# Earlier loads and clears, an overlapped first count tile, and edge groups of three in a graph layer kernel

## What is computed

```python
xn = layernorm(x)
# two graph convolutions; A counts the edges src->dst, plus one self loop for each node
def gcn_conv(x, W, b):                       # deg: edges and loop that end in a node
    norm = dinv[src] * dinv[dst]             # dinv = 1 / sqrt(deg)
    return segment_sum((x @ W.T)[src] * norm, dst) + b
gnn = gcn_conv(relu(gcn_conv(xn, W1, b1)), W2, b2)
# linear attention with exponential features, 12 heads of 64, 256 features
mix = layernorm(xn + attention(xn) @ W_proj + b_proj) * gamma + beta
x = x + gnn + mix
x = x + expert_ffn(layernorm(x))             # 8 experts, one chosen per row
```

## Time and profile before

| what | us |
|---|---|
| median of three runs | 2721.11 (2715.38 to 2743.76) |
| the profiled execution's own time | 2723.26 |
| its span | 2721.5 |
| PE busy | 2408.9 |
| DVE busy | 1390.2 |
| ACT busy | 798.5 |
| POOL busy | 796.1 |

### The profile page before, as it was taken

How to read it: one execution, slowest core, us unless ns; L and a number is a source line. 1 busy time by engine, 2 the same in 40 slices (tenths; PEclk the granted TensorE clock), 3 DMA queues, 4 the chain that set the end, 5 groups by cost and what they waited for, 6 DMA issues and landing times. The chain is left out here.

```text
span 2721.5 us, 44665 instructions
## 1 busy us (share of the span) xinstructions
PE 2408.9 (89%) x16483; PEld 1629.3 (60%) x16483; DVE 1390.2 (51%) x2868; ACT 798.5 (29%) x1090; POOL 796.1 (29%) x562
## 2 busy tenths in 40 slices
PE   2888989999999999998892899999998889999476
PEld 1666858676866666665561466666664556666354
DVE  5565848584666766765210444444441334444343
ACT  2223424332364654743110222222220001111132
POOL 1115444444455555554554000000000000000265
PEclk9989999999999999999996899999998999999688
DMA  5995545454412123123212666666656655444185
GB/s 216 384 380 143 136 127 136 133 152 111 119 1 59 1 58 58 0 59 67 61 0 54 221 215 215 218 220 217 218 196 224 216 171 168 169 167 162 42 162 107
DMA packets 161756, 392.18 MB, mean 144 GB/s; under 512 B 74832, under 2 KB 81850, under 8 KB 152028
## 3 DMA queue, kind: packets, MB, share of 16 engines
q1 hardware_dynamic: 77196, 299.90, 32.2%
q0 software_dynamic: 73632, 61.04, 12.9%
q10 hardware_dynamic: 10800, 29.50, 2.8%
HBM read 226.03 MB, written 169.83 MB: 145 GB/s over the span
## 5 line engine op out<-in xcount | busy, mean ns | idle before, releaser
L364 PE MATMUL pair<-arena 128*128 128x384 f16 (+2 forms) x5760 | 905.6, 319 | 25.0 <-SPq L353 7.9
L1744 PE MATMUL pair<-arena 128*128 128x384 f16 x4900 | 822.8, 328 | 84.1 <-DVE arena L1332 57.6
L675 POOL DMA_INDIRECT cells<-arena x392 | 637.3, 1626 | 631.5 <-DMA cells<-arena 456.3
L364 PEld LDWEIGHTS pair<-arena 128*128 128x128 f16 (+1 forms) x5760 | 566.9, 99 | 349.1 <-issue 25.1
L1744 PEld LDWEIGHTS pair<-arena 128*128 128x128 f16 x4900 | 476.6, 98 | 396.1 <-DVE arena L1332 58.0
L707 POOL DMA_INDIRECT slots<-arena x25 | 29.0, 1159 | 1022.2 <-DVEq L1447 1006.1
L1567 PE MATMUL pair<-arena 128*128 128x256 f32 x600 | 168.9, 416 | 17.5 <-ACT arena L779 17.5
L1578 PEld LDWEIGHTS pair<-arena 128*128 128x128 f32 x1200 | 159.6, 201 | 27.3 <-ACT arena L803 22.0
L1578 PE MATMUL pair<-arena 128*128 128x66 f32 x1200 | 159.3, 282 | 17.7 <-ACT arena L803 17.6
L1123 DVE SCALAR_TENSOR_TENSOR arena<-arena 128x256 f16<-128x256 f32 x392 | 161.8, 480 | 4.7 <-DVE arena L1051 4.4
L803 ACT ACTIVATE arena<-pair 128x512 f32<-128x512 f32 x150 | 87.2, 590 | 170.4 <-PE pair L1567 167.1
(11 more groups left out here) (191 smaller groups left out, 2274.0 us busy)
## 6 DMA issues: line engine op xcount, KB each, us to landing
cells<-arena POOLq DMA_DIRECT2D x25, 1600.0 KB, 11.6
arena<-cells SPq DMA_DIRECT2D x25, 1600.0 KB, 9.1
ahl_dram<-arena SPq DMA_DIRECT2D x25, 1600.0 KB, 12.4
arena<-ahl_dram SPq DMA_DIRECT2D x25, 1600.0 KB, 7.8
arena<-in_x SPq DMA_DIRECT2D x70, 384.0 KB
arena<-key_dram SPq DMA_DIRECT2D x28, 896.0 KB
split_w<-arena SPq DMA_DIRECT2D x32, 384.0 KB
arena<-split_w SPq DMA_DIRECT2D x32, 384.0 KB, 5.6
```

What stands on the lines that cost most here:

```text
L364: ins = nc.tensor.matmul(dst[half], left(k, a), right(k, b, half), start=start and n == 0, stop=stop and n == 2)
L675: nc.gpsimd.indirect_dma_start(cells, bass.IndirectOffsetOnAxis(ap=idx_all[:, m:m + 1], axis=0), val_all[:, m:m + 1], None, bounds_check=C ...
L1744: ins = nc.tensor.matmul(pair[u][:, half, 0:HD], a[:, 0, s * P:(s + 1) * P], X[part][:, s, half * HD:(half + 1) * HD], start=(s == 0 and p ...
```

## The change

It has five parts.

1. **Start.** All six weight blocks have their own staging place and are loaded at once. `consts` is raised to 1 as soon as the identity matrix is there, and only PE waits for that; DVE and ACT wait for the rest (`consts` 2) later. ACT loads its table early. Lo parts are transposed into bank 6, and ACT evicts the first three of them (`LO_ACT`).
2. **Clear.** The zero fill starts when the last weight block has landed, instead of when it has been split. The zeros' place moves from `xT`'s fourth chunk to its fifth.
3. **Loops.** The 24 DMAs of self loops go. POOL adds the identity to the diagonal block of each table tile in SBUF, for tiles 14 to 24; ACT's `counts` waits for `loops`. The reduction for the flag moves ahead of the last two scattered units.
4. **First count tile.** `xT` is laid out by chunk, so the first table tiles can be loaded while later first rows are made: tile 0 when 5 tiles are done, tile 1 when 10 are. `counts(0)` of ACT and DVE stands between first rows 22 and 23.
5. **Groups of three.** `EPU` = 15 and `G` = 3. 27 units have edges: 405 columns in 135 groups, where there were 392 in 196. Each scan is 128x384. The mask `earlier` is float16.

```diff
-EPU = 14
+EPU = 15
-G = 2
+G = 3
...
+LO_ACT = 3
...
-        earlier = small(G, G * P)
+        earlier = small(G, G * P, dt=F16)
...
-        zeros = at(RT + 960, 640)
+        zeros = at(RT + 4 * 3840, 640)
...
+        xT = arena[:, RT:RT + 2 * K * C * HW].bitcast(F16).rearrange("p (c m n) -> p c m n", c=C, m=2 * K)
...
         def staged(m):
-            return at(WST + 1536 * (m % 2), 2, D)
+            return at(WST + 1536 * m if m < 2 else RT + 3840 + 1536 * (m - 2), 2, D)
...
             def load_weights(m):
-                if m >= 2:
-                    sp.wait_ge(w_lo_done, m - 1)
...
+            sp.wait_ge(scattered, 16 * ET_EDGES)
+            for u in range(2):
+
+                sp.wait_ge(z1_full, TC * (u + 1))
+                sp.dma_start(a_in[u], cells_t[u]).then_inc(a_ld[u], 16)
             sp.wait_ge(z1_full, T)
             sp.dma_start(rw_raw, ffn_in[:, HB:HB + NX].rearrange("(k p) e -> p k e", p=P)).then_inc(consts_in, 16)
             fetch_split(sp, G2_AT, 1, g2_in)
-            sp.wait_ge(scattered, 16 * ET_EDGES)
-            for u in range(2):
-                sp.dma_start(a_in[u], cells_t[u]).then_inc(a_ld[u], 16)
...
-            pool.wait_ge(w_lo_done, K)
+            pool.wait_ge(X_in[C - 1], 16)
...
-            pool.wait_ge(cleared[0], 16 * ((T + 1) // 2 + T - FIRST_LOOP // P))
             for b in range(EDGE_UNITS):
+                if b == EDGE_UNITS - 2:
+                    pool.wait_ge(flag_max, 1)
+                    nc.gpsimd.partition_all_reduce(flag_f[:, 1:2], flag_f[:, 0:1], P, bass.bass_isa.ReduceOp.max)\
+                        .then_inc(flag_max, 1)
                 scatter(b)
...
+            for n in range(T):
+                own = a_in[n % 2][:, n * P:(n + 1) * P]
+                pool.wait_ge(a_ld[n % 2], 16 * (n // 2) + 16)
+                if n < FIRST_LOOP // P:
+                    pool.sem_inc(loops, 1)
+                else:
+                    nc.gpsimd.tensor_tensor(own, own, ident_end if n == FIRST_LOOP // P else ident, ALU.add)\
+                        .then_inc(loops, 1)
...
-            counts(0, 0)
+            for n in range(4):
+                first_rows(n, n, 0)
+            with dve.Fori(1, 5) as i:
+                for q in range(4):
+                    first_rows(4 * i + q, q, i)
+            for n in range(20, T):
+                if n == T - 2:
+                    counts(0, 0)
+                first_rows(n, n % 4, n // 4)
```

More of the change, by code:

```diff
@@ L66, in over_tiles @@
         body(2 * i + 4, 0, i + 2)
[L69 to L76, removed]
 def reused(i):
@@ L187, in build, with xT_cols, xT_tile @@
         eint = [at(RX + 8880 + ET * i, ET, dt=I32) for i in range(8)]
-        krow, ktmp = at(RX + 1200, ET), at(RX + 1620, ET)
-        xT = [at(RT + 9600 * part, K, NP, dt=F16) for part in range(2)]
+        krow, ktmp = at(RX + 1200, ET), at(RX + 1660, ET)
+        xT = arena[:, RT:RT + 2 * K * C * HW].bitcast(F16).rearrange("p (c m n) -> p c m n", c=C, m=2 * K)
+        def xT_cols(c, k, part, first, n):
+            if isinstance(c, int):
+                return xT[:, c, part * K + k, first:first + n]
+            return xT[:, bass.ds(c, 1), part * K + k, first:first + n].rearrange("p a b -> p (a b)")
+        def xT_tile(n, part):
+            return xT[:, n // TC, part * K:(part + 1) * K, n % TC * P:(n % TC + 1) * P]
         qs = [at(RX + 1200 + CW * u, 2, CW, dt=F16) for u in range(2)]
@@ L273, in build @@
         Q_AT, P_AT, G1_AT, G2_AT, FFN_AT = range(0, 5 * K, K)
-        w_in_sem = [sem("w_in0"), sem("w_in1")]
+        X_in = [sem(f"X_in{c}") for c in range(C)]
+        w_in_sem = [sem("w_in0")] + X_in
         pre_in, pre_hi, pre_lo, pre_st = [sem(f"pre_{n}") for n in ("in", "hi", "lo", "st")]
@@ L411, in build @@
         sq_asked, sq_done, flag_max = sem("sq_asked"), sem("sq_done"), sem("flag_max")
-        X_in = [sem(f"X_in{c}") for c in range(C)]
         z1_full, X_hi, X_lo = sem("z1_full"), sem("X_hi"), sem("X_lo")
         a_ld, a_st = [sem("a_ld0"), sem("a_ld1")], [sem("a_st0"), sem("a_st1")]
+        loops = sem("loops")
         counts_hi, counts_lo, g_full = sem("counts_hi"), sem("counts_lo"), sem("g_full")
@@ L1371, in layer1 @@
                 residual(n, u, i)
-            counts(0, 0)
+            for n in range(4):
+                first_rows(n, n, 0)
+            with dve.Fori(1, 5) as i:
+                for q in range(4):
+                    first_rows(4 * i + q, q, i)
+            for n in range(20, T):
+                if n == T - 2:
+                    counts(0, 0)
+                first_rows(n, n % 4, n // 4)
+            cs = Chain(dve, dve_done, links(1))
+            dve.wait_ge(flag_max, 2)
+            cs.link(nc.vector.tensor_scalar(flag_i, flag_f[:, 1:2].to_broadcast([P, 2]), COUNT_EXACT, None, ALU.is_gt))
+            dve.sem_inc(flag_max, 1)
             dve.wait_ge(rw_hi_done, 1)
@@ L1522, in turn, with turn_part @@
                 return ins
[L1524 removed]
+            def turn_part(part, b=7):
                 for k in range(K):
[L1526 removed]
+                    ins = nc.tensor.transpose(bank16(b)[:, k * P:(k + 1) * P], part[:, k * P:(k + 1) * P], ident)
                 return ins
@@ L1719, in _ @@
             pe.wait_ge(g1_in, 16 * K)
-            def node_tile(n):
-                return lambda k, part: xT[part][:, k, bass.ds(n * P, P)]
-            def first_rows(n, q, i):
-                if reused(i):
+            for n in range(T):
+                q = n % 4
+                if n >= 4:
                     pe.wait_ge(X_lo, n - 3)
```

104 lines of the change are left out of this document (48 added, 56 removed).

## The result

The changed kernel takes 3096.55 us (median of 4, 3092.58 to 3100.38); the kernel before took 2722.46 in runs on the same chip (median of 4, 2715.38 to 2743.76). The ratio is 1.136 [1.129, 1.142]: 374 us slower, where the forecast was 2698.

The account below looks back on a forecast made before the run. The prediction took a ring of scan, DMA, ACT and DVE to pace the chunk stage, with PE idle at the start and ahead of layer 1. Terms -21 - 54.6 - 2 + 55 = -23 gave 2698 us, range 2670 to 2718.

Parts of the forecast that it names:

- what would show it: The prediction's list of signs expected in the new trace, among them later layers, experts and attention unchanged.
- Start, -21: Before PE's first v product: earlier weight loads and constants bring it 21 us forward, between 17 and 24.
- First count tile, -54.6: Ahead of layer 1: PE's wait falls from 57.6 us to 3, as the count tile is made between first rows.
- Groups of three, +55: In the chunk stage: wider scans lengthen each unit by about 2.55 us, a loss of 55 us in all.
- the term for that: In the chunk stage: more PE idle time can lower the granted clock at more chunk starts, +3 us.
- The ring: Chunk stage: scan, key load, block store and load, then ACT and DVE set the pace, 16.17 us per unit.
- the hidden scan: Rival, chunk stage: the longer scan fills DVE's idle time, only some 15 us are lost; 2658 us, chance 0.13.
- the fast mask: Rival, chunk stage: the float16 mask speeds the scan to 5.3 us per unit; 2640 us, chance 0.03.
- the failed overlap: Rival, ahead of layer 1: groups of three land much later, so PE waits as before; 2755 us, chance 0.03.
- Clock, -2: Start of layer 1: with less idle time ahead, the first 110 products run faster, 2 us of 3 taken.
- The scatter, 1190 to 1360: POOL's last scatter in groups of three was expected between 1190 and 1360 us, over 100 us of cover.
- POOL's additions at nothing: POOL's 11 new additions to the diagonal were costed at nothing; under 15 us in all if cover fails.

Follow-up runs that it names:

- E1: The changed kernel with the fill edges given a destination that no node's degree counts: 2706.35 us, 0.985 of the kernel before.
- E2: The kernel before with the limit for low-part products at 550 instead of 2048, so that they run: 3139.04 us, ratio 1.144, one run.
- E5: E1 with the first table tiles' loads and the first count tile put behind the last first row: 2720.41 us, 0.991 of the kernel before.
- E4: E1 in groups of two again (EPU 14, G 2): 2708.47 us, 0.985 of the kernel before.
- E8: The kernel before with one tiny POOL addition behind the all-reduce of the flag: 2727.22 us, ratio 0.994, one run.
- E9: The kernel before with SyncE issuing the weight split step ahead of its wait for the scan: 2721.13 us, ratio 0.989.
- E11: The kernel before with groups of three, the float16 mask, tiles moved to make room and fill edges uncounted: 2752.21 us, ratio 1.002.
- E12: E11 with SyncE issuing the weight split step ahead of its wait for the scan: 2685.28 us, 0.981 of the kernel before.
- E7: E1 with SyncE issuing the weight split step ahead of its wait for the scan: 2646.35 us, 0.963 of the kernel before.

## Why the prediction was wrong

**The step that failed** is the premise in "what would show it": "Layer 1, layer 2, the experts and the attention unchanged". The change was followed through the order of instructions and through shapes, and no instruction of layer 1 moves. What changed is a value. Raising `EPU` was priced as longer scans, wider tables and key loads; that `ET * P` also sets how many fill edges there are, that they all have one destination, and that the degree they make is compared with 2048 was not followed. Everything needed stood in the sources: 4401 against 2048, and a branch of 50 products for each tile and layer. From the earlier trace rows, whose first 110 products of layer 1 took 20.94, even the price was at hand: 2500 x 0.165 to 0.190 = 412 to 475 us; measured 414.3. No rival had it: the slowest that any of them gives is 2755.

**Without that step** the range would have held. E1 is the changed kernel with the branch off: 0.985 [0.980, 0.990] of before, where 2670 to 2718 is 0.981 to 0.999 of 2721.1. The forecast itself, 2698, is 0.991, and E1 gained more than that, 40 us where 23 were forecast; on its chip the wait ahead of layer 1 that the change removes was longer in the one execution that shows it (75.61 in E2). Term by term, in the changed kernel's own trace:

- *Start, -21:* 34.69 against 56.61, so -21.9. Right, and inside 17 to 24. The identity came at 1.8 and not at 13.3, since POOL's 11.27 us gap went too. That was not foreseen, but at 13.3 it would have been in time too: PE's first transpose starts at 14.77, behind ACT's first hi part.
- *First count tile, -54.6:* 3.33 is left of 57.62, so -54.3. The size is right, the reason half so: E5 shows that the overlap alone carries 14 to 18 of it, and the rest needs the scatters to end early, which only the groups of three do (E4: 79.48 us of wait with the overlap in place). The working had both, "this needs the scatter to end before about 1490", but credited the gain to one edit and the loss to the other.
- *Groups of three, +55:* PE's first rows end at 1482.9 instead of 1447.8, +35.1; with the 21.9 of the start that is +57.0 for the stage. The copies say 58.7 (687.7 against 629.0). The sum is right and its parts are less so: with the rest of the change in place the threes cost 67.7 (E1 against E4), and the rest of the change, the earlier fill among it, gives 9.1 of the stage back (E4's 619.9 against 629.0). The granted clock of the stage fell from 0.95 to 0.90, and PE was busy 29 us longer for the same products (595.3 against 566.1), so slower products are part of the loss; the term for that was 3. The scan instruction repeats every 0.54 us (0.546 expected), the second chunk's copies stand 18.5 to 18.8 apart (18.3 to 18.8 expected). The ring was the right picture, and the hidden scan, the fast mask and the failed overlap are out: no gain from float16, since the scan is 614 ns for 384 columns.
- *Clock, -2:* the first 96 products of layer 1 took 18.52, 0.193 each, no better than 0.190 in the earlier trace rows. The gap ahead of them had shrunk from 57 to 3.3 us and the granted clock in it was 0.82 where it was 0.52. But in the first 3.8 us of layer 1 it was 0.50, as in the first 3.6 before, and only then rose. This term was wrong.
- *The scatter, 1190 to 1360:* 1358, at the late edge; 8.8 per group, where 8.7 was worked out.
- *POOL's additions at nothing:* 11 of them, 4.7 us in all, none on the path.

The sum, -23, measured -19.2 at the start of layer 1.

## What to carry to other kernels

When a size changes, follow it into the data as well as into the shapes: padding, counts and flags are computed from it, and a branch that was never taken leaves no row in the trace to be seen in. List each conditional block of the program with what its condition compares, and price it as a rival. And where two chains end close together, an edit that shortens one and lengthens the other shows no gain by itself (1.002), nor does one that shortens only the chain that ends first show much (0.989), so weigh such edits together (0.981, and 0.963 with all).

## What the runs showed of the hardware

- Once a partition all-reduce has run, the next POOL operation that is neither a memset nor a DMA stands behind idle time that the trace doesn't name. In E8 it is 9.26 us, ahead of the added operation. Where the all-reduce was the last such operation of the program, the idle time is at the start of the execution, ahead of the first affine_select: 11.27 to 12.37 us in the kernel before, E2, E9, E11 and E12, and 0.50 in all other kernels here. That something of POOL's code stays loaded from one execution to the next is an inference; only the gaps are shown. The Trainium skill, page GPSIMD Engine Reference, section on instruction dispatch, speaks of a load of about 6 us, with no instruction in the profile, at the first call to a freshly loaded routine. The 5.90 us ahead of the all-reduce agree with that (5.89 in E8); the gaps behind it are half as long again, up to twice that.
- DVE's scan with a float32 and a float16 source repeats every 0.54 us at 384 columns (614 ns for one) and every 0.416 at 256: 1.0 ns per column, so the float16 mask does not raise the rate.
- The mean granted clock from the first to the last copy of the chunk stage was 0.95 in the kernel before, with PE idle in 10% of it, 0.90 in the changed one (13%), 0.93 in E7 (9%) and 0.98 in E9 (5%).
- A short gap ahead of layer 1 didn't speed up its first products. 110 of them took 20.94 us behind 57.6 idle (the kernel before), 20.79 behind 3.3 (E1), and 19.41 behind 20.1 (E12).
